# Two attention layers whose rows and probabilities are split in fp16 halves and then transposed by DMA transfers

## What is computed

```python
q, k, v = heads(h @ Wq + bq), heads(h @ Wk + bk), heads(h @ Wv + bv)      # h: relu(layernorm(x)), 12 heads of 32
scores = einsum('bhqd,bhkd->bhqk', q, k) * scale + bias_from(adj)
probs = softmax(scores, axis=-1)
out = einsum('bhqk,bhkd->bhqd', probs, v)                                  # L3: out @ Wo.T + bo
```

## Time and profile before

| | |
|---|---|
| median of 3 runs | 2785.4 us (2784.74 to 2786.96) |
| the profiled execution's span | 2784.9 us |
| PE busy | 2508.1 us (90%) |
| DVE busy | 2456.0 us (88%) |
| ACT busy | 1806.0 us (65%) |
| POOL busy | 1450.3 us (52%) |
| SP's transfers | 73936 packets, 59.54 MB, 7.1% of 16 engines |

### The profile page before, as it was taken

The page is one execution under the profiler, slowest core; times in us unless marked ns, Lnnn a source line. Parts: engine busy times, 40 slices in busy tenths (PEclk is TensorE's granted clock), DMA queues, the critical chain, the costliest instruction groups (busy, mean ns, idle before and its releaser), DMA issues. The chain is left out here.

```text
span 2784.9 us, 89934 instructions
## 1 busy us (share of the span) xinstructions
PE 2508.1 (90%) x29505; PEld 1866.2 (67%) x29505; DVE 2456.0 (88%) x9771; ACT 1806.0 (65%) x4409; POOL 1450.3 (52%) x2016
## 2 busy tenths in 40 slices
PE   5898898886999998799999999999968998899987
PEld 4888788874666664566666666666557777777776
DVE  6989989886999999688888888888869999999998
ACT  5888888874555554455555555555547777777775
POOL 1223233224777777477777777777633444344433
PEclk9999999998999999799999999999989999999998
DMA  3001011002000000100000000000000000000000
GB/s 104 28 29 30 26 30 30 26 14 88 9 9 9 9 9 6 47 10 9 9 9 10 9 9 9 9 10 9 8 9 25 23 23 26 23 23 23 26 23 23
DMA packets 73989, 60.21 MB, mean 22 GB/s; under 512 B 7888, under 2 KB 73936, under 8 KB 73936
## 3 DMA queue, kind: packets, MB, share of 16 engines
q1 hardware_dynamic: 73936, 59.54, 7.1%
HBM read 46.92 MB, written 12.58 MB: 21 GB/s over the span
## 5 line engine op out<-in xcount | busy, mean ns | idle before, releaser
L149 PE MATMUL bank<-L_w_hi,L_hT_hi 128*128 128x384 f16 x2112 | 691.7, 328 | 0.0
L151 PE MATMUL bank<-L_w_hi,L_hT_lo 128*128 128x384 f16 x2112 | 691.4, 327 | 0.0
L150 PE MATMUL bank<-L_w_lo,L_hT_hi 128*128 128x384 f16 x2112 | 691.4, 327 | 0.0
L550 ACT ACTIVATE raw_weights<-L_minus_scores,L_minus_max 128x128 f32<-128x128 f32 x1536 | 475.7, 389 | 71.2 <-DVE L_minus_max L663 71.2
L149 PE MATMUL bank<-L_hT_hi,L_w_hi 128*128 128x128 f16 x2304 | 418.4, 222 | 1.2 <-issue 0.8
L150 PE MATMUL bank<-L_hT_lo,L_w_hi 128*128 128x128 f16 x2304 | 418.3, 222 | 0.0
L151 PE MATMUL bank<-L_hT_hi,L_w_lo 128*128 128x128 f16 x2304 | 418.1, 222 | 0.0
L663 DVE CUSTOM_DVE_ANT_0 L_minus_scores<-bank,L_minus_score_bias 128x128 f32<-128x128 f32 x1536 | 348.0, 283 | 0.4 <-issue 0.4
L1085 ACT ACTIVATE L_e<-bank,L_nmax 128x128 f32<-128x128 f32 x192 | 70.6, 368 | 365.0 <-DVE L_nmax L1170 365.0
L151 PEld LDWEIGHTS bank<-L_w_hi,L_hT_lo 128*128 128x128 f16 x2112 | 207.4, 98 | 138.2 <-issue 2.5
L150 PEld LDWEIGHTS bank<-L_w_lo,L_hT_hi 128*128 128x128 f16 x2112 | 207.6, 98 | 108.5 <-issue 2.0
(11 more groups left out here) (171 smaller groups left out, 7853.5 us busy)
## 6 DMA issues: line engine op xcount, KB each, us to landing
adj_tile<-in_adj SPq DMA_DIRECT2D x320, 64.0 KB, 1.7
x<-in_x SPq DMA_DIRECT2D x64, 192.0 KB, 2.3
out<-L_result SPq DMA_DIRECT2D x64, 192.0 KB, 1.9
raw_weights<-in_L_gnn_Wq SPq DMA_DIRECT2D x2, 576.0 KB, 4.1
raw_weights<-in_L_gnn_Wk SPq DMA_DIRECT2D x2, 576.0 KB, 5.8
raw_weights<-in_L_gnn_Wv SPq DMA_DIRECT2D x2, 576.0 KB, 5.5
raw_weights<-in_L_gnn_Wl SPq DMA_DIRECT2D x2, 576.0 KB, 4.7
raw_weights<-in_L_gnn_Ws SPq DMA_DIRECT2D x2, 576.0 KB, 4.9
```

The lines of the kernel that those rows point to most:

```text
L149: pe.matmul(out, stat[0], move[0], start=first, stop=False)
L150: pe.matmul(out, stat[0], move[1], start=False, stop=False)
L151: return pe.matmul(out, stat[1], move[0], start=False, stop=last)
L550: last = act.activation(probs[:, n_.slot(k), i, :], scores[:, i, :], ACT.Exp, bias=nmax[:, n_.slot(k), i:i + 1], scale=-1.0)
```

## The change

Rows, probabilities and, in L3, the attended rows are split into fp16 halves before the transposition, in SBUF: ACT copies the high half, POOL (rows) or the DVE (probabilities, attended rows) subtracts for the low half, into `h16`, `p16` and `o16`, where both halves lie side by side. SP then issues a transposing transfer (`dma_start_transpose`) from there to `hT`, `pT` and `oT`: one of 128x768 for the rows, one of 128x1024 for each third of the probabilities, one of 128x768 for the attended rows. TensorE's transposes in the two layers and the DVE's `turned_lo` are gone. The pipeline is one step longer: rows are normalised for n+3, the products with probabilities are of n-2, the output of L3 is of n-3. The orders of DVE, ACT, PE, POOL and SP are rewritten; `p16` and `pT` exist once, `h16` and `hT` twice, `result` once instead of twice.

```diff
@@ tiles, banks, phases
-                hT = [sb(s, f"{tag}_hT_{a}", [P, 2, D], F16) for a in ("hi", "lo")]
+                h16 = sb(s, f"{tag}_h16", [P, 2, 2, D], F16)
+                hT = sb(s, f"{tag}_hT", [P, 2, 2 * C, P], F16)
...
-                pT = [sb(s, f"{tag}_pT_{a}", [P, H, P], F16) for a in ("hi", "lo")]
+                p16 = sb(s, f"{tag}_p16", [P, C, 2, HC, P], F16)
+                pT = sb(s, f"{tag}_pT", [P, C, 2 * HC, P], F16)
...
-                pT_banks, s_banks = banks[0:3], banks[0:4]
+                s_banks = banks[0:4]
                 q_bank, k_bank = banks[4], banks[5]
-                pv = banks[4][:, 0:H * (HD + 1)].rearrange("p (h e) -> p h e", h=H)
-                v_bank, oT_bank = banks[6], banks[6]
-                hT_bank, o_bank = banks[7], banks[7]
-                phase = Phase(G, first=4, after=2) if last_layer else Phase(0, last=4, after=2)
+                v_bank, o_bank = banks[6], banks[6]
+                pv = banks[7][:, 0:H * (HD + 1)].rearrange("p (h e) -> p h e", h=H)
+                phase = Phase(G, first=4, last=4, after=3) if last_layer else Phase(0, first=4, last=4, after=3)
@@ SP
+                        def turn_h(n_, k):
+
+                            wait_apart(sp, (hT_ready, n_.done(k - 1, 16)), (h16_lo, n_.done(k)), (v_psum, n_.done(k - 2)))
+                            sp.dma_start_transpose(hT[:, n_.slot(k), :, :],
+                                                   h16[:, n_.slot(k), :, :].rearrange("p a n -> p (a n)")).then_inc(hT_ready, 16)
+
+                        def turn_probs(n_, k, c):
+
+                            wait_apart(sp, (pT_ready[c], n_.done(k - 1, 16)), (p16_lo[c], n_.done(k)), (pv_psum, n_.done(k - 1)))
+                            sp.dma_start_transpose(pT[:, c, :, :],
+                                                   p16[:, c, :, :, :].rearrange("p a h n -> p (a h n)")).then_inc(pT_ready[c], 16)
...
                             if isinstance(n_.t, int) and n_.t == 0:
                                 if not last_layer:
                                     load_x(n_, 0)
                                     load_x(n_, 1)
+                                    load_x(n_, 2)
+                                turn_h(n_, 0)
+                                turn_h(n_, 1)
+                                if not last_layer:
                                     weights.load(sp)
...
                                 load_adj(n_, 2)
+                                turn_h(n_, 2)
+                            if n_.has(-1):
+                                for c in range(C):
+                                    turn_probs(n_, -1, c)
+                            if last_layer and n_.has(-2):
+                                turn_o(n_, -2)
@@ POOL
+                        def h_low(n_, k):
+
+                            wait(pool, h16_hi, n_.done(k))
+                            pool.tensor_tensor(h16[:, n_.slot(k), 1, :], h[:, :], h16[:, n_.slot(k), 0, :],
+                                               ALU.subtract).then_inc(h16_lo, 1)
...
+                            if n_.has(3):
+                                norm(n_, 3)
+                            if last_layer and n_.has(-3):
+                                add_out_bias(n_, -3)
+                            if n_.has(3):
+                                h_low(n_, 3)
                             if last_layer and n_.has(0):
                                 fold_scores(n_)
+                            if not last_layer and n_.has(-2):
+                                add_to_x(n_, -2)
@@ ACT
                         def p_split(n_, k, c):
-                            wait(act, pT_psum[c], n_.done(k))
-                            act.activation(pT[0][:, HC * c:HC * c + HC, :],
-                                           pT_banks[c][:, :].rearrange("p (h q) -> p h q", h=HC), ACT.Copy).then_inc(pT_hi[c], 1)
+                            wait_apart(act, (probs_ready[c], n_.done(k)), (pT_ready[c], n_.done(k - 1, 16)))
+                            act.activation(p16[:, c, 0, :, :], probs[:, n_.slot(k), HC * c:HC * c + HC, :],
+                                           ACT.Copy).then_inc(p16_hi[c], 1)
@@ DVE
-                        def turned_lo(n_, k):
-                            wait(dve, hT_hi, n_.done(k))
-                            dve.tensor_tensor(hT[1][:, n_.slot(k), :], hT_bank[:, 0:D], hT[0][:, n_.slot(k), :],
-                                              ALU.subtract).then_inc(hT_lo, 1)
...
-                            wait(dve, pT_hi[c], n_.done(k))
-                            hs = slice(HC * c, HC * c + HC)
-                            dve.tensor_tensor(pT[1][:, hs, :], pT_banks[c][:, :].rearrange("p (h q) -> p h q", h=HC),
-                                              pT[0][:, hs, :], ALU.subtract).then_inc(pT_lo[c], 1)
+                            wait(dve, p16_hi[c], n_.done(k))
+                            dve.tensor_tensor(p16[:, c, 1, :, :], probs[:, n_.slot(k), HC * c:HC * c + HC, :],
+                                              p16[:, c, 0, :, :], ALU.subtract).then_inc(p16_lo[c], 1)
@@ TensorE
-                        def turn_probs(n_, k, c):
-                            wait(pe, probs_ready[c], n_.done(k))
-                            for j in range(HC):
-                                mm = pe.transpose(pT_banks[c][:, c128(j)], probs[:, n_.slot(k), HC * c + j, :], ident[:, :])
-                            mm.then_inc(pT_psum[c], 1)
-
                         def attend(n_, k):
                             wait(pe, v_lo, n_.done(k))
+                            wait(pe, attended_ready, n_.done(k - 1))
                             for c in range(C):
-                                wait(pe, pT_lo[c], n_.done(k))
+                                wait(pe, pT_ready[c], n_.done(k, 16))
...
                             if n_.has(0):
                                 score(n_)
-                            if last_layer and n_.has(-2):
-                                turn_o(n_, -2)
+                            if n_.has(-2):
+                                attend(n_, -2)
+                            if n_.has(0):
+                                project_v(n_, 0)
                             if n_.has(1):
-                                wait(pe, attended_ready, n_.done(-2))
+                                wait(pe, q_lo, n_.done())
+                                wait(pe, k_lo, n_.done())
                                 project_turned(n_, 1, 0, q_bank, q_psum)
                                 project_turned(n_, 1, 1, k_bank, k_psum)
-                            if last_layer and n_.has(-2):
-                                project_out(n_, -2)
-                            if n_.has(0):
-                                wait(pe, max_ready[C - 1], n_.done())
-                            if n_.has(-1):
-                                for c in range(C):
-                                    turn_probs(n_, -1, c)
-                            if n_.has(0):
-                                project_v(n_, 0)
-                            if n_.has(2):
-                                turn_h(n_, 2)
-                            if n_.has(-1):
-
-                                if n_.has(1):
-                                    wait(pe, q_lo, n_.done(1))
-                                wait(pe, attended_ready, n_.done(-2))
-                                attend(n_, -1)
+                            if last_layer and n_.has(-3):
+                                project_out(n_, -3)
```

More of the change, by code:

```diff
@@ L591, in step @@
                                     exponents(n_, -1, c)
-                            if last_layer and n_.has(-2):
-                                o_split(n_, -2)
+                                for c in range(C):
+                                    p_split(n_, -1, c)
+                            if n_.has(0):
+                                v_split(n_, 0)
                             if n_.has(0):
@@ L638, in score_bias @@
                         def score_bias(n_, k):
+                            wait(dve, max_ready[C - 1], n_.done(k - 2))
                             a = adj_tile[:, n_.slot(k), :]
@@ L731, in add_result @@
                             wait(dve, xsum_ready, n_.done(k))
-                            wait(dve, out_written, n_.done(k - 2, 16, base=0))
-                            dve.scalar_tensor_tensor(out=result[:, n_.slot(k), :], in0=o_bank[:, 0:D], scalar=unscale[:, 3:4],
+                            wait(dve, out_written, n_.done(k - 1, 16, base=0))
+                            dve.scalar_tensor_tensor(out=result[:, :], in0=o_bank[:, 0:D], scalar=unscale[:, 3:4],
                                                      in1=xsum[:, :], op0=ALU.mult, op1=ALU.add).then_inc(result_ready, 1)
@@ L737, in step @@
                             if isinstance(n_.t, int) and n_.t == 0:
-                                for k in (0, 1):
```

(16 more changed lines are left out.)

165 lines of the change are left out of this document (73 added, 92 removed).

## The result

The changed kernel takes **2974.2 us** (median, 2972.4 to 2975.4) against 2785.8 us beside it: 1.0678 times the kernel before, 95% interval 1.0663 to 1.0693. My forecast of 2833 us had the direction and its range held the time, but the loss is 188 us and not 48.

The account below looks back on a forecast made before the run. It took SP's transfer queue to bound L0 (10.0 instead of 9.08 us a step, +59 us) and the DVE L3 (-30 us); with +18 us once, +48 us in all gave 2833 us, range 2690 to 3250 us.

Parts of the forecast that it names:

- What bounds the kernel: Both attention layers: the DVE bounds, TensorE is second, so taking transposes off TensorE is worth nothing by itself.
- The sum: Whole kernel: L0 +59 us, L3 -30 us, once-only +9 and +9 us; in all +48 us, giving 2833 us.
- the quick rival: Transposing transfers as quick as a copy, T 0.9 to 1.3 us: about 2705 us, 2690 to 2780; chance 0.35.
- T: Time of one 256 KB unit of transposing transfer on SP's queue, taken as 1.79 us.
- my piece count: Transfer engines: a unit is 1024 pieces of 256 bytes over 16 engines, 64 x 28 ns = 1.79 us.
- The signs I gave: After the change: 3.2 us to landing, TensorE waiting about 2 us a step, SP's longest wait not for the DVE.
- The queue's loop: L0, v to v through SP's in-order transfers and probability products: 3.75 T + 3.3 us, 10.0 us a step.
- this loop and TensorE's: L0: the loop through SP's transfers, 10.0 us, and beside it one through TensorE's score, products and projections, 8.0 us.
- The rival at 0.04: L0: TensorE's clock falls to 1.2 GHz, +1.8 us a step, +115 us, 2948 us; chance 0.04.
- The port rival: L3: POOL's SBUF reads hold the DVE through a shared port, step 11.7 us, +48 us, 2911 us; chance 0.06.
- Once-only terms: Outside the steps: late weights at the start +9 us, both layers draining one step later +9 us.
- The weights' 9 us: Start: weight loads stand behind the first transposes on SP, asked for at about 15 instead of 5.96 us: +9 us.

Follow-up runs that it names:

- e9_before_order: The kernel before, with the DVE's three small instructions on score sums in L3 moved between the maxima, away from POOL's sums: 2758.1 us.
- e3_fill: The changed kernel with x loaded one graph earlier and 24 unread TensorE products per step of L0: 2852.6 us.
- e10_v_only: The changed kernel with TensorE's projection of v ahead of the products with probabilities, x loaded as late as in the changed kernel: 2974.3 us.
- e7_weights_first: The changed kernel with L0's weight loads ahead of the first two transfers of rows on SP: 2974.0 us.

## Why the prediction was right and where it failed

**What bounds the kernel.** For L3 right: with nothing but the DVE's row shortened (`e9_before_order`) the step fell. For L0, and that TensorE's transposes alone are worth little, no run tests it.

**The sum.** Against it L0's steps cost 148.5 us and not 59, L3's gave 5 and not 30, and what lies outside the steps cost 45 and not 18. (My terms add up to +47 and not +48, and those of the quick rival to a band of 2704 to 2798 and not 2690 to 2780. Nothing here hangs on either.)

**T.** The unit was mis-sized: 1.79 us forecast, 1.36 measured, between a plain copy (0.91) and my piece count. That is the ground of the quick rival, below its deciding point of 1.54, and by my own rule L0 should have been at 8.4 us. It went to 11.5, so by my own test (a step changed by over 1 us with T under 1.5) I was wrong in kind. The signs I gave misled: landing took 3.3 us, which I had put down to my T, and SP's longest wait is no longer for the DVE but for v of TensorE (102.7 against 32.2 us in 200 to 550 us), as forecast. One sign did speak against my loop: TensorE waits 0.5 us a step for the transfers and not 2. Landing holds more than T; the rate is read from issues in a row.

**The queue's loop.** Its form was right, its constant short. In `e3_fill`, at full clock, it is 9.4 us: rows' transfer to the first third 1.4, two issues 2.8, landing 3.1, products 0.3, v 1.6, semaphore 0.1 (medians). My 3.75 T + 3.3 gives 8.4 at T = 1.36. The landing beyond T is 1.8 us and not 1.4; the rows' transfer holds the queue for 1.4 us and not 0.75 T = 1.0, as its issue is nearly as long as that of 256 KB; v and the 1.40 us from issue to issue make the rest.

**The step that failed** is the one after it, that this loop and TensorE's were the only ones. The change moves the load of x behind the three new transfers in SP's row and lets the DVE's statistics, ahead of the maxima, wait for it. I costed what the new transfers wait for, and put what waits behind them at nothing. The kernel's text shows it: SP comes to `load_x(n_, 3)` right behind `turn_probs` of the step before, and the DVE's `stats(n_, 3)` wants it in the same step. What the runs show in its place: the loop through the load of x is 11.5 us, 64 x 2.4 = 150 us; with only the load one graph earlier the kernel is 81.6 us faster, where the next loop holds it, and with only v moved it is as slow as before. With these 150 us in place of L0's 59, the sum would have been 2924 us.

**Clock.** The rival at 0.04 was half right: v does run at 1.2 GHz in L0 (0.79 on average). In the changed kernel it should cost nothing, as v isn't on the loop that sets the step (`e10_v_only`; no run raises the clock there). Once x is early, extra products that raise the clock bring 40 us.

**L3.** Forecast 10.5 us; measured 11.12 in the median and 10.98 on average, where it was 10.96 and 11.06, so -5 us over the layer instead of -30. The port rival, at 0.06, had the mechanism: POOL's sums cost 0.94 us a step, and both its signs are there, DVE instructions that end with POOL's and 12 columns that take over 1 us. By the number its 11.7 is no nearer than my 10.5. Neither figure asks what becomes of the 1.3 us a step that the kernel before already paid there. In 2300 to 2850 us the test for zero is down from 1.02 to 0.32 us, while the attended rows' low half is up from 0.53 to 0.91, the kept rows (L713) from 0.62 to 0.84, the row scales from 0.23 to 0.41 and the bias from 0.22 to 0.34: mostly the price changed hands. I had seen its row and given it too little. The DVE was over 97% busy, as said. The Trainium skill states in "SBUF — State Buffer", on the shared pair of ports, that a DVE instruction with two inputs in SBUF and a GpSimd one that reads SBUF can't run side by side, and that the later one is blocked until the other's whole instruction ends. The trace agrees for L713, which has two such inputs: 12 columns took 792 ns on average with POOL's sums and 201 without. The row that I named for it in the prediction, L675, reads only one tile, and was held all the same.

**Once-only terms.** +18 forecast, 45 measured outside the steps. The weights' 9 us were wrong (`e7_weights_first`). Why the first maximum still comes 5 us later there was not tried. The longer pipeline makes most of the rest: 36 maxima, three graphs' worth, stand ahead of the first reciprocal where it was 24, so each layer has one step more, and I had counted only some transfers in series. In L0 the time from the first maximum to the first reciprocal is 33.1 us instead of 14.7, in L3 23.3 instead of 15.0. The other 6 us on the way to L3 were not traced.

**Against a plain copy.** Transposing transfers from SBUF to SBUF move 256 KB in 1.36 us here, 193 GB/s, and this kernel's plain loads, of pieces of 512 and 1536 bytes, 256 KB in 0.91 us. The Trainium skill ("Advanced Engine Details and Errata", X-Bar Transpose) puts both at the same speed; here the measurement decides, and it says 1.5 times the time of a plain load.

## What to carry to other kernels

A transfer added to an in-order queue delays every load behind it: for each load, ask who consumes it in the same step and what that engine has queued behind the wait, and write the loop out. Data that depends on nothing can be loaded one step earlier; do that before you judge such a change. A longer pipeline costs a whole step in each layer. And when POOL holds up the DVE, place POOL's long reads of SBUF beside the DVE's reads of PSUM: here that order gave 95 us.

## What the hardware showed unasked

- An issue of a transposing transfer holds SP for 1.21 us (128x768) or 1.25 us (128x1024), against 0.35 for a plain one, and the next of three starts 1.40 us after the one before. Landing is 2.8 and 3.3 us.
- Giving TensorE products that nobody reads made kernels faster twice, by 40 and 23 us, as the granted clock rose (0.83 to 0.99 and 0.92 to 1.00 in 200 to 550 us).
- POOL holds up not only the DVE's two-tile instructions: a one-input 128x128 fp32 instruction went from 196 to 780 ns. The statistics (547 ns) and the maxima, which read PSUM (0.28 us), are as long beside POOL as apart from it.
